# Row maxima of an attention pipeline run 44 units (28 in the second layer) ahead of the scores

## The reference

```python
# layer 1: eight batches, 16 heads of 8 features, no mask
scores = einsum('bshd,bthd->bhst', q, k) / sqrt(8)
a = softmax(scores); o = einsum('bhst,bthd->bshd', a, v)
# ... projection, layernorm, feed-forward, layernorm; times silu of
#     a mixture of 16 experts, each token sent to one of them (at most 256 tokens each)
# layer 2: the same size, causal with a linear bias by distance,
#     times silu of a mixture of 8 experts, each token sent to two
out = x + attention(layernorm(x)) * silu(experts(layernorm(x)))
```

## Time and profile before

| | us |
|---|---|
| median of 3 runs | 1188.52 |
| lowest and highest | 1180.65, 1189.01 |
| the profiled execution | 1175.42 |
| its span, first to last instruction | 1173.5 |

### The profile page before, as it was taken

How to read it: one execution, slowest core, us unless ns; L and a number is a source line. 1 busy time by engine, 2 the same in 40 slices (tenths; PEclk the granted TensorE clock), 3 DMA queues, 4 the chain that set the end, 5 groups by cost and what they waited for, 6 DMA issues and landing times.

```text
span 1173.5 us, 22918 instructions
## 1 busy us (share of the span) xinstructions
PE 1005.4 (86%) x7466; PEld 543.6 (46%) x7466; DVE 787.6 (67%) x2434; ACT 646.6 (55%) x1252; POOL 576.8 (49%) x670
## 2 busy tenths in 40 slices
PE   4757889998989898887988877777999899899888
PEld 2522269633333333332423444445888654444434
DVE  5597833488788887878777755674444587788741
ACT  1204732476767677665757643454444477667665
POOL 5266600155546373728678887741000264545564
PEclk8657989999999999999989988887999999999988
DMA  5852457662414050412323142234888544354221
GB/s 146 203 157 65 127 161 210 212 155 47 100 36 111 9 125 15 100 37 56 99 60 99 39 117 58 47 95 134 247 245 248 145 114 120 82 125 108 69 59 46
DMA packets 121864, 129.81 MB, mean 111 GB/s; under 512 B 13920, under 2 KB 104864, under 8 KB 121536
## 3 DMA queue, kind: packets, MB, share of 16 engines
q1 hardware_dynamic: 115184, 115.37, 37.9%
q0 software_dynamic: 6144, 12.60, 4.2%
q10 hardware_dynamic: 432, 0.52, 0.2%
HBM read 82.54 MB, written 52.35 MB: 115 GB/s over the span
## 4 chain that ended last, share of the span: by engine, by line
PE 56%; DVE 15%; issue 8%; POOL 7%; DMA 6%; ACT 4%; another core or an unknown queue 1%; SPq 1%; POOLq 0%; DVEq 0%; ACTq 0%
PE ps_banks L588 7%; PE ps_banks L629 7%; PE ps_banks L1810 5%; PE ps_banks L634 5%; DVE a_neg_max L888 4%; PE ps_banks L595 4%; DVE a_masked L894 3%; PE ps_banks L674 3%; PE ps_banks L1548 3%; PE ps_banks L1823 2%; PE ps_banks L1562 2%; PE ps_banks L726 2%; POOL sent L1673 2%; PE ps_banks L732 2%; PE ps_banks L640 2%
## 5 line engine op out<-in xcount | busy, mean ns | idle before, releaser
L777 ACT ACTIVATE a_probs<-ps_banks 128x512 f32<-128x512 f32 x512 | 278.9, 600 | 125.2 <-PE ps_banks L588 119.8
L588 PE MATMUL ps_banks<-q_strip,k_strip 53*128 53x512 bf16 (+3 forms) x1024 | 280.3, 352 | 67.5 <-DVE a_neg_max L888 24.4
L888 DVE TENSOR_REDUCE a_neg_max<-ps_banks 128x1 f32<-128x512 f32 x448 | 283.4, 682 | 63.8 <-PE ps_banks L595 57.2
L595 PE MATMUL ps_banks<-k_strip,q_strip 51*128 51x512 bf16 (+3 forms) x1024 | 289.2, 364 | 23.9 <-DVE a_neg_max L885 15.9
L894 DVE CUSTOM_DVE_ANT_0 a_masked<-ps_banks,mask_wide 128x384 bf16<-128x384 f32 (+3 forms) x512 | 223.8, 487 | 83.5 <-PE ps_banks L595 72.8
L779 ACT ACTIVATE a_probs<-ps_banks 128x512 f32<-128x512 f32 x256 | 144.5, 603 | 86.9 <-PE ps_banks L546 76.7
L1078 POOL DMA_INDIRECT tokens<-made,at x96 | 93.2, 971 | 178.1 <-DMA made<-work 126.0
L588 PEld LDWEIGHTS ps_banks<-q_strip,k_strip 53*128 53x128 bf16 x1024 | 72.6, 95 | 162.4 <-issue 60.3
L629 PE MATMUL ps_banks<-a_probs,v_aug 128*32 128x512 f32 x1024 | 139.7, 618 | 0.3
L595 PEld LDWEIGHTS ps_banks<-k_strip,q_strip 51*128 51x128 bf16 x1024 | 72.6, 95 | 131.3 <-ACT a_probs L777 62.4
L545 PE MATMUL ps_banks<-mask_kq,ident_halves 64*128 64x256 bf16 (+1 forms) x320 | 80.2, 261 | 0.3 <-issue 0.3
(11 more groups left out here) (259 smaller groups left out, 1753.2 us busy)
## 6 DMA issues: line engine op xcount, KB each, us to landing
work<-in_pack SPq DMA_DIRECT2D x39, 450.0 KB, 3.4
q_rows<-a_q_parts SPq DMA_DIRECT2D x96, 128.0 KB
k_rows<-a_k_parts SPq DMA_DIRECT2D x96, 128.0 KB
q_strip<-q_rows SPq DMA_DIRECT2D x64, 192.0 KB
k_strip<-k_rows SPq DMA_DIRECT2D x64, 192.0 KB
work<-in_w SPq DMA_DIRECT2D x32, 256.0 KB, 3.1
sent<-in_zeros SPq DMA_DIRECT2D x14, 512.0 KB, 8.0
work<-sent SPq DMA_DIRECT2D x55, 128.0 KB, 3.2
```

Source lines behind the costliest of these rows:

```text
L588: mm = pe.matmul(sbank[:, at:at + hi - lo], k_now[rows(js, ROW_END), slot, kt * P:(kt + 1) * P], q_now[rows(js, ROW_END), slot, lo:hi], st ...
L595: mm = pe.matmul(mbank[:, at:at + hi - lo], q_next[rows(jm, ROW_SHIFT), slot, qt * P:(qt + 1) * P], k_next[rows(jm, ROW_SHIFT), slot, lo:h ...
L777: act.activation(probs[si // 4 % 2][:, si % 4, :], bank, ACT.Exp).then_inc(sems["probs"], 1)
L888: dve.tensor_reduce(neg_max[:, half, qt, hd:hd + 1], bank, AX.X, ALU.max, negate=True).then_inc(sems["max_out"], 1)
```

## The change

The maxima no longer begin with the stage. `LEAD = (44, 28)`: in stage b the first 20 units (12 in layer 2) hold the last 20 (12) maxima of batch b itself, and the units after that the first 44 (28) of batch b+1. Stage -1 keeps 44 units, the others keep their number; stage 15, which had no maxima, has 12. `minus` and `shift` of each half move with the maxima they belong to. The first half of a batch's rows is shifted at u54 (u33) where it was u44 (u24), the second half at u22 (u16) where it was u4 (u3) of the next stage. The stores of query and key rows leave the steps `q` and `k` and become a step `rows` behind the second half's `shift`. The first half's `fetch` moves from u32 to u44 (u23 to u28). In stage -1 the steps `slots0`, `weigh0` and `send0` get other places.

```diff
+LEAD = (44, 28)
-    0: {0: [("zTa", 2)], 1: [("ln3a", -2), ("zT", 2)], 2: [("shift", 0, 1)], 3: [("ln3b", -2), ("norm", -1, QT - 1)], 4: [("q", 2)],
+    0: {0: [("zTa", 2)], 1: [("ln3a", -2), ("zT", 2)], 3: [("ln3b", -2), ("norm", -1, QT - 1)], 4: [("q", 2)],
-        10: [("ln1", -1), ("z", 1)], 11: [("logits", -2)], 12: [("gather", -1), ("norm", 0, 0)], 16: [("yT", -1), ("fetch", 2, 0)],
+        10: [("ln1", -1), ("z", 1)], 11: [("shift", 0, 1), ("logits", -2)], 12: [("rows", 2), ("gather", -1), ("norm", 0, 0)], 16: [("yT", -1)], 22: [("fetch", 2, 0)],
-        22: [("shift", 1, 0)], 23: [("gate", -1), ("ff2a", -1)], 24: [("ff2", -1)], 25: [("tanh", -1), ("fmom", -1, 0)], 26: [("fmom", -1, 1)],
-        27: [("ln2", -1), ("norm", 0, 2), ("gz", -1)], 29: [("mix", -1)], 31: [("store", -1)]},
+        27: [("shift", 1, 0), ("ln2", -1), ("norm", 0, 2), ("gz", -1)], 29: [("mix", -1)], 31: [("store", -1)]},
-    scores = UNITS[layer(0)] if live(0) else 0
-    maxima = UNITS[layer(1)] if live(1) else 0
-    units = max(scores, maxima)
+    own = [(0, m) for m in range(LEAD[layer(0)], UNITS[layer(0)])] if live(0) else []
+    ahead = [(1, m) for m in range(LEAD[layer(1)])] if live(1) else []
+    units = max(scores, len(own) + len(ahead))
+        md, mi = own[u] if u < len(own) else (1, None)
+        if ahead and u >= len(own):
+            at, left = u - len(own), units - len(own)
+            if (at + 1) * len(ahead) // left > at * len(ahead) // left:
+                md, mi = ahead[at * len(ahead) // left]
+        steps.append(("unit", 0, (si, mi, layer(md), md), layer(0)))
-                        if name in ("q", "k"):
+                        if name == "rows":
                             wait(sp, sems["strips1"], n.at("strips1"))
-                            wait(sp, sems["split"], n.at("split") + 1)
-                            order = (0, 0, 0, 1, 1, 2) if name == "q" else (0, 1, 2, 0, 1, 0)
-                            for a in range(PARTS):
-                                sp.dma_start(dram[name][par][:, a, :, :],
-                                             parts[name][:, order[a], :]).then_inc(sems[f"{name}_out"], 16)
+                            for i, (k, order) in enumerate((("q", (0, 0, 0, 1, 1, 2)), ("k", (0, 1, 2, 0, 1, 0)))):
+                                wait(sp, sems["split"], n.at("split") - 1 + i)
+                                for a in range(PARTS):
+                                    sp.dma_start(dram[k][par][:, a, :, :], parts[k][:, order[a], :]).then_inc(sems[f"{k}_out"], 16)
```

More of the change, by code:

```diff
@@ L154 @@
 LAST0 = {
-    **MISC[0], 12: [("gather", -1)], 16: [("fetch", 2, 0)], 17: [("yT", -1)], 18: [("ff1", -1, 0)], 19: [("ff1", -1, 1)], 20: [("ff1", -1, 2)], 21: [("ff1", -1, 3)],
-    27: [("ln2", -1), ("gz", -1)], 29: [], 30: [("mix", -1)],
+    **MISC[0], 12: [("gather", -1)], 16: [], 17: [("yT", -1)], 18: [("ff1", -1, 0)], 19: [("ff1", -1, 1)], 20: [("ff1", -1, 2)], 21: [("ff1", -1, 3)],
+    27: [("shift", 1, 0), ("ln2", -1), ("gz", -1)], 29: [], 30: [("mix", -1)],
 }
@@ L320, in plan @@
         si = u if u < scores else None
-        mi = u * maxima // units if maxima and (u + 1) * maxima // units > u * maxima // units else None
-        if maxima == units:
-            mi = u
-        steps.append(("unit", 0, (si, mi, layer(1)), layer(0)))
+        md, mi = own[u] if u < len(own) else (1, None)
[4 more added lines that the diff above has]
+        steps.append(("unit", 0, (si, mi, layer(md), md), layer(0)))
         if scores and u - 1 in late and ends_quad(late[u - 1][1], layer(late[u - 1][0])):
@@ L327, in plan @@
             add("take", d, g // (QT if layer(d) == 0 else 3))
-        if mi is not None and (mi + 1) % (maxima // 2) == 0:
-            add("minus", 1, mi // (maxima // 2))
+        if mi is not None and (mi + 1) % (UNITS[layer(md)] // 2) == 0:
+            add("minus", md, mi // (UNITS[layer(md)] // 2))
         if scores and u in late:
             total(*late[u], RING)
-        while place < PLACES and (place + 1) * units <= (u + (2 if scores == maxima == UNITS[0] else 1)) * PLACES:
+        while place < PLACES and (place + 1) * units <= (u + (2 if scores == len(own) + len(ahead) == UNITS[0] else 1)) * PLACES:
             misc(place)
@@ L354, in adds @@
         "norm": {**both, "dve": 1}, "zTa": {}, "zT": both,
-        "q": {**both, "split": 1, "pool": 3, "q_out": 16 * PARTS}, "k": {**both, "split": 1, "pool": 3, "k_out": 16 * PARTS},
+        "q": {**both, "split": 1, "pool": 3}, "k": {**both, "split": 1, "pool": 3}, "rows": {"q_out": 16 * PARTS, "k_out": 16 * PARTS},
         "v": both, "z": both, "shift": {**both, "shift_in": 64}, "minus": {"dve": 1, "minus": 1},
@@ L573, in _ @@
                         if name == "unit":
-                            si, mi, max_layer = arg
-                            q_now, k_now, q_next, k_next = q_strip[par], k_strip[par], q_strip[1 - par], k_strip[1 - par]
+                            si, mi, max_layer, max_d = arg
+                            max_par = (b + max_d) % 2
+                            q_now, k_now, q_next, k_next = q_strip[par], k_strip[par], q_strip[max_par], k_strip[max_par]
                             sbank, mbank = banks[:, n.at("scores") % RING, :], banks[:, MAX_BANK + n.at("max_in") % RING, :]
```

7 lines of the change are left out of this document (4 added, 3 removed), and 4 rows, old and new, of the table EXTRA.

## The result

The changed kernel takes 1226.92 us (1226.52 to 1228.15, 4 runs) against 1185.34 us for the kernel before, a ratio of 1.0358 with an interval of 1.0325 to 1.0391. The forecast was 1197 us with 1173 to 1208 us as its range, so the time lies well outside. The profiled execution of the changed kernel has a span of 1225.3 us, 51.8 us longer than that of before.

A forecast was written before the change was run, and what follows sets the result against it. PE was taken as the bound inside the stages, POOL's sends up to the first expert. Terms -1.1 + 5.0 - 1.7 + 4.8 + 1.6 = +8.6 us on 1188.5 us gave 1197.1 us; range 1173 to 1208 us, forecast's own 1190 to 1203.

The forecast's parts named there:

- Start: Stage -1 and stage 0: first exponential 11.4 us sooner, but POOL's chain to the experts only 1.1 us sooner; term -1.1 us.
- Stores and fetch: Row stores behind SP's second-half shift and the later fetch, in both layers: they would cost nothing.
- The 4.8 us from shift to landing: Layer 2, second half: hand-over 1.3, last issue 1.83 and landing 1.7 us, against 3.2 us of PE's own way to u20.
- the term of layer 1, +5.0 us: Stages 1 to 6: eleven claims behind moved shifts at 0.9 us each, less 3.2 us, three quarters kept: +5.0 us.
- at its old places the shift itself waited for ACT ... those go: Stages 1 to 6: the old shifts' waits for ACT, 1.2 and 2.0 us, would vanish, a gain of 3.2 us.
- a quarter of the sum: Stages 1 to 6: a quarter of 6.7 us taken off, since a later PE waits less on DVE (20.9 us).
- used it only as a gain: Clock rival, stage 15: PE ran at 0.55 before; with 12 maxima it may stay at 1.00, saving up to 5 us; chance 0.05.
- Layer 2, +4.8 us: Stages 10 to 14: u20 waits 1.6 us for shifted rows, less 0.65 us of old shift wait, in each of five stages.
- The rival of late rows: Layer 2: shifted rows land after 6.0 us, 2.1 us lost per stage, first half late too; +20 us, 1208 us; chance 0.20.
- Stages 8 and 9: nothing: Layer 2's first stages: units take longer there, so the shifted rows arrive in time; no cost.
- Stage 7: 8 fewer maxima on the array half their neighbour uses, 0.21 us each: -1.7 us.
- Stage 15: u20 waits 1.6 us for shifted rows with nothing to give back, the 12 maxima costing nothing: +1.6 us.

The follow-up runs named there:

- e4: Kernel before with only the new stores of query and key rows and the later fetch, maxima and shifts as before: ratio 1.0027 to the kernel before.
- e9: e4 with only the shifts of layer 1 moved to u22 and u54, order of maxima as before: ratio 1.0121 to the kernel before.
- e8: Changed kernel with SP issuing the first four loads of layer 2 experts' weights ahead of stage 9's first-half shift: ratio 1.0208 to the kernel before.
- e13: e12 with a layer 2 lead of 38 for 37: ratio 1.0101 to the kernel before.
- e10: Kernel before with slots0, weigh0 and the first groups of sends three to five places sooner in stage -1: ratio 1.0021.
- e5: Changed kernel with maxima ahead in layer 2 alone and its second half's shift behind u13 for u16: ratio 1.0041 to the kernel before.
- e12: e4 with maxima running ahead by LEAD = (60, 37), all shifts at their old places: ratio 1.0271 to the kernel before.

## Why the prediction was wrong

**What held.** Start: the first exponential came 8.8 us sooner (11.4 expected) and nothing of it reached the first expert, because POOL's chain sets that; the change of the chain's start was 0.86 us for 1.1. Stores and fetch cost nothing that a run can tell (e4). The new waits are where the forecast put them: `logits` and `norm` on ACT's copy, 0.7 to 0.8 us each for 0.9, and u20 of layer 2 on the landing, 1.0 to 1.4 us a stage with `norm`'s 0.3 us beside it, for 1.6. The 4.8 us from shift to landing measured 5.0 us.

**The step that failed: the term of layer 1, +5.0 us.** It was 24.0 us in the first comparison and 16.2 us on chip 3. The claims themselves were right: eleven waits with 7.4 us for the 9.9 us forecast. What was taken off them, and what was left out, was wrong. First, "at its old places the shift itself waited for ACT ... those go": 3.2 us were taken as a gain. But e9, which removes the shifts from u4 and u44, runs level with e4 up to u20 and gains 0.1 to 0.2 us at u44. At its old places the shift cost next to nothing, neither its waits nor its own 0.38 us; at u22 and u54 it cost some 1.0 us each in e9. And at u22 the shift still waited, now for DVE (2.2 us in six waits).

Second, "a quarter of the sum" for waits on DVE that shrink: these fell by 2.5 us (20.9 to 18.4 us, stages 1 to 7), but the waits on ACT's exponentials rose by 4.8 us, so nothing was won.

Third, a wait was priced at its own length. At a clock of 1.00 a stage of layer 1 lost 2.1 us, near to the 2.5 us that PE loses at the two places, against 0.8 us forecast; where the clock fell it lost 3.0 to 4.6 us. PE's busy time in stages 1 to 6 grew by 9.3 us in the first comparison and by 5.7 us on chip 3 for the same matmuls, 35 to 40% of the loss of this layer. That share isn't firm: e4 and the kernel before differ by 2.6 us in it at the same length, and e9 has none of it (346.06 us for e4's 347.98) and still takes 10.2 us more. I had read in the earlier trace rows a stretch at clock 0.55 in stage 15 and used it only as a gain.

**Layer 2, +4.8 us, was mis-sized**: 14.1 us in the first comparison, 9.4 us on chip 3. The late landing was right: on chip 3 the exponentials lose 1.6 to 1.8 us between u16 and u20. But some 0.5 us a stage at the first half's shift (u33, two units behind its `minus`) were not costed. The saving of 0.65 us a stage showed as 0.5 us at u6, and in stages 10 to 13 about 0.1 us of it was left at u10. The landing was guessed from a wrong reading: 48 KB is not the smallest transfer whose landing the trace gives. The same list has a load of 4 KB (`gate_b`) that lands after 3.6 us, though from device memory at the start of the program; the landing here took at most 2.2 us. The rival of late rows, with 2.1 us a stage, came nearer to the time, but not by its mechanism: the landing ended after 5.0 us, not after 6.0. Its late u0 can't be told apart, since the kernel before has waits of 1.2 and 1.0 us at a u0 as well. "Stages 8 and 9: nothing" was wrong for the wait: u20 of stage 8 waited 2.23 us in the first comparison and in the repeats, though that stage as a whole got no longer (-1.9 us, and -0.4 us on chip 3).

**Stage 9, 0 us forecast, +6.1 us.** The step missing is the queue of SP: I had asked what a moved shift holds up among the stores, not that the experts' weights stand behind the last shift of stage 9. e8 shows that the order alone isn't the price: beside the sends the 1.8 MB of weights lengthen the sends' wait, ahead of the tokens they lengthen the tokens', so 3.6 us are taken from one wait and 2.7 us given to another. The size isn't settled either. In the repeats the stage took 184.5 and 186.1 us for 182.7 us, 1.8 and 3.4 us more.

**Stages 7 and 15.** Stage 7 was forecast at -1.7 us and measured +5.3 us in the first comparison and -1.9 us on chip 3. It can't be read: that stage varies from 62.6 to 71.2 us between kernels on chip 4, with its clock. The term had its count of neighbours right (12 maxima on the busy half for 20), but left out that the stage now has 48 maxima for 40, and the claim behind its own shift (`logits`, 1.0 us). Stage 15, forecast at +1.6 us, took 3.7 us more in the first comparison and 0.9 us less on chip 3, with a wait of 1.0 to 1.2 us at u20.

**The start, -1.1 us, was +0.5 us**, and +1.9 us on chip 3, where the first expert came 2.6 us later than before. In the first comparison the six transfers of sends on the chain took 23.9 us in sum for 21.1 us, so that the chain ended 2 us later. Why they took longer isn't settled.

**The range.** The bounds of the terms add up to 1186 to 1207 us, not to the 1190 to 1203 us that were given, and both end under the measured time.

**What stays open.** The first comparison lost 3.6%, the repeats on two chips 2.3%. In its trace the exponentials lose 1 to 4 us more between u28 and u40 in stages 1, 3 and 4, and PE's list has `ff1` (L730) waiting for ACT's copy for 6.1 us in five waits of stages 1 to 6, up to 3.0 us at once. The kernel before, in the same comparison, has 2.5 us in four waits at that step that no engine explains. In stage 1 ACT itself stood still for 3.53 us ahead of that copy, and its row names no engine that it waited for. In the traces on chip 3 it waits 1.4 us in six waits, up to 0.2 us each, with and without the change. Whether the chip or the occasion made the difference is not known. Nor is it settled which part of e13's 1.0% is the clock's.

None of the kernels beats the kernel before. The nearest were e10 (1.0021) and e4 (1.0027).

## What to carry to other kernels

A helper step in a full pipeline has a place, not only a cost: the same shift was free at u4 and cost 1.0 us at u22 (e9), and 1.3 us at u13 in layer 2 (e5), so a plan that moves work must list, for each resource it claims (a bank, a queue, an array half), who stands directly ahead and behind. Before a stretch is shortened, follow the chain that leaves it: 8.8 us won in stage -1 were paid back in full at the next join. And give a new wait of TensorE a range that reaches above its length where it runs close to full: here a stage lost 2.1 us where the clock held and 3.0 to 4.6 us where it fell.

## What the runs showed of the hardware

Two bf16 matmuls on opposite halves of the array ran together (both started at 975.73 us, 0.39 us each), on one half one after the other (0.23 us apart). With all 40 pairs of a stage on one half (e12), PE's busy time in stages 10 to 13 was 155.36 us for 136.97 us in e13, and the stages were 3.9 us longer each.

Four row transfers of 4 KB took 2.43 us to issue from 1023.16 us on; the last began some 1.83 us later (an estimate from four equal issues), and PE went on at 1027.15 us, so the landing took at most 2.2 us, with twelve stores behind them on the queue. The forecast took 1.7 us from a transfer of 48 KB.

The same change on the same program cost 3.6% in one comparison and 2.3% in two others on chips 9 and 3, where the kernel before was 3% faster. On chips 3, 4 and 9 the kernel before had medians within 0.7 us of each other.
